# Attention scores with the keys in the partitions: four heads in row bands of TensorE, sums and outputs in column bands

## The chip, the cores and the metric

The kernel runs on one core of a Trainium2 chip. The metric is the device time of one execution in microseconds (us). Engines: PE is TensorE (matrix products), PEld its weight loads, DVE is VectorE, ACT is ScalarE, POOL is GpSimd, SP issues DMAs. Each engine works through its own queue in order, and semaphores tie the queues together.

## The reference

Input `x` is 4 x 2048 rows of 512, `ctx` 4 x 77 rows of 384.

```python
q = (layernorm(x) @ Wq + bq)        # 16 heads of 32
k = ctx @ Wk + bk;  v = ctx @ Wv + bv
attn = softmax(q @ k.T / sqrt(32))   # per head, over the 77 keys
out = attn @ v                       # back to 512 columns
x = x + relu(out @ W1 + b1) @ W2 + b2
# then: layernorm, one of 8 experts by argmax of logits, gelu MLP of that expert, added to x
```

All is fp32. Most products are made in three TensorE passes: each operand is split into a rounded part (high, type fp32r) and the rest (low), and high x high, high x low and low x high are added in PSUM.

## The kernel before

The 8192 rows are worked in 16 blocks of 512 (b = 0 to 15), each as 4 sub-blocks of 128 rows (s). A list of steps, `sched`, is written out by hand; every engine walks it and issues what the step holds for it, so this list sets the order in every queue. PSUM has 8 banks; a program gives each step of PE the bank that is free longest, and `own_bank` makes PE wait until that bank's last reader is done.

In a block, XT transposes the normalised rows, Q makes the queries with features in the partitions (4 tiles m of 128 features, which are 4 heads each, so a group g of heads is a tile), S makes scores for a group and a sub-block with 128 rows in the partitions and 4 x 77 = 308 columns, against a block-diagonal key tile `kbd`. DVE takes the maxima; ACT makes exponentials with the sum (groups 0 and 2), or DVE subtracts and ACT makes them at once (1 and 3). DVE takes sums and a reciprocal of 16 columns, POOL multiplies. PT transposes the probabilities with PE in 5 chunks for a pair of groups, ACT and DVE split them into high and low, and AV multiplies them with a block-diagonal `vbd`; OUT splits the result into `actA`. H and Y are the two products of the MLP (H in 8 tiles m of 12 matmuls; Y of one sub-block in two halves, YA and Y, of 12 matmuls each). TT transposes the result rows of the block before for its expert logits.

The scores of block b + 1 lie in the order between the halves of Y of block b, and PT, AV and H of a block follow after them. After the 16 blocks the experts' stage works through 71 tiles of 128 rows; the change doesn't touch it.

Of the kernel before, what the change touches and what calls it, by code (L numbers as in the profile page):

```python
# [18 lines left out]
F32 = mybir.dt.float32  # L19
# [33 lines left out]
PH = 2 * HG  # L53
CH = [128, 128, 128, 128, 104]
NC = len(CH)
VR = [min(P, NB * M - i) for i in range(0, NB * M, P)]
NV = len(VR)
CA, CC, CB = (0, 1), (2,), (3, 4)
# [9 lines left out]
PIECES = []  # L68
for _h in range(PH):
    for _c in range(NC):  # L70
        _a, _z = max(M * _h, P * _c), min(M * _h + M, P * _c + CH[_c])
        if _a < _z:
            PIECES.append((_c, _a - P * _c, _a - M * _h, _z - _a, _h))


def xattn_moe_kernel(nc, A, out):
    region = nc.dram_tensor("region", [NE * REG + P, ROW], F32).ap()
    k_parts = nc.dram_tensor("k_parts", [P, 2, KD, NB * M], F32).ap()
    v_parts = nc.dram_tensor("v_parts", [NB * M, 2, D], F32).ap()
# [26 lines left out]
    vbd, vbd_at = sb("vbd", [P, 2, NP, NC, P], F32R)  # L106
    kbd, _ = sb("kbd", [P, 2, KD, SCP], F32R)
    E, E_at = sb("E", [P, NP, SUB, 2 * SC])
# [20 lines left out]
    mx, _ = sb("mx", [P, KD * SUB, HG])  # L129
    sm, _ = sb("sm", [P, KD, SUB * HG])  # L130
    rc, _ = sb("rc", [P, KD, SUB * HG])
# [26 lines left out]
    def staged(name, shape, dt=F32):  # L158
# [6 lines left out]
    assert o[0] <= E_at + size([P, KD, SUB, SC], F32)  # L165
# [3 lines left out]
    v_f = [staged(f"v_f{i}", [P, D]) for i in range(2)]  # L169
# [3 lines left out]
    k_hl = staged("k_hl", [P, 2, KD, NB * M], F32R)  # L173
    k_f = staged("k_f", [P, KD, NB * M])
    assert o[0] <= actH_at + size([P, 2, SLOTS, BLK], F32)
# [3 lines left out]
    assert NV == 3 and VR[0] >= M  # L179
    v_hl = [at(f"v_hl{i}", [P, 2, D], F32R, (rows_at[1], xn_at)[i // 2] + i % 2 * size([P, 2, D], F32))  # L180
            for i in range(NV)]
    assert 2 * size([P, 2, D], F32) <= min(size([P, SUB, ROW], F32), SUB * size([P, D], F32))
# [5 lines left out]
    b2e = at("b2e", [P, NE, D], F32, vbd_at)  # L188
    assert 4 * NE * D <= size([P, 2, KD, SCP], F32) + size([P, 2, NP, NC, P], F32)
# [28 lines left out]
    assert o[0] <= E_at + size([P, KD, SUB, SC], F32)  # L218
# [25 lines left out]
    with ExitStack() as ctx:  # L244
        bank = [ctx.enter_context(nc.psum_tensor(f"bank{i}", [P, 512], F32)) for i in range(8)]

        def sem(name):
# [7 lines left out]
        st_k, st_v, ld_k, ld_v = sem("st_k"), sem("st_v"), sem("ld_k"), sem("ld_v")  # L255
# [7 lines left out]
            "dve_bks pe_k act_kf act_k dve_k pe_v dve_vf act_v dve_v pool_zero dve_const "  # L263
            "act_wq dve_wq act_w1 pool_w1 act_w2 dve_w2 act_kbd dve_tri "
            "dve_xn pool_xb pe_xT act_xT dve_xT pe_q act_q dve_q pe_s dve_max dve_sub act_es act_exp dve_rc pool_p "
            "pe_pt act_pt dve_pt pe_av act_c dve_c act_o dve_o pe_h act_h dve_h pe_y dve_x2 dve_row pool_ones pe_gate dve_gate "
# [12 lines left out]
        def attention_tail(b):  # L279

            for c in range(NC):
                step("PT", b, 0, c)
            if b:
                step("SUM", b, KD - 1)
            for c in CA:
                step("PT", b, 1, c)
            if b:
                step("TT", b - 1, 0)  # L290
            step("AV", b, 0, "C")
            step("COPY", b, 0)
            step("AV", b, 0, "A")
            step("AV", b, 0, "B")
            if b:
                step("TT", b - 1, 1)
            step("AV", b, 1, "A")
            step("ADD", b, 0, "A")
            step("ADD", b, 0, "B")
            step("OUT", b, 0, "A")  # L300
            for c in CC + CB:
                step("PT", b, 1, c)
            if b:
                step("TT", b - 1, 2)
            step("AV", b, 1, "C")
            step("OUT", b, 0, "B")
            step("COPY", b, 1)
            step("AV", b, 1, "B")
            step("ADD", b, 1, "A")
            step("ADD", b, 1, "B")  # L310
            step("OUT", b, 1, "A")
            step("OUT", b, 1, "B")
            if b:
                for s in range(SUB - 1):
                    step("TTOUT", b - 1, s)
            else:
                for i in (1, 2):
                    step("VHI", i)
                for i in (1, 2):
                    step("VLO", i)  # L320
                    step("VSTORE", i)

# [4 lines left out]
        step("BKS")  # L327
        step("DRAIN")
# [6 lines left out]
        step("KP", 3)  # L335
        for m in range(KD):
            step("KLO", m)
        step("KSTORE")
# [3 lines left out]
        step("KCOPY")  # L342
# [4 lines left out]
        step("VHI", 0)  # L347
        step("VLO", 0)
        step("VLOAD", 0, 0)
        step("VLOAD", 0, 1)  # L350
        step("VSTORE", 0)
        step("CONV_W1", 0)
        step("Q", 0, 1)


        for s in range(SUB - 1):
            step("S", 0, 0, s)
        step("QLO", 0, 1)
        step("Q", 0, 2)
        step("S", 0, 0, SUB - 1)  # L360
        step("CONV_W1", 1)
        for s in range(SUB):
            step("S", 0, 1, s)
        step("QLO", 0, 2)
        step("EXP", 0, 1)
        step("Q", 0, 3)
        step("SUM", 0, 0)
        for s in range(SUB):
            step("S", 0, 2, s)
        step("QLO", 0, 3)  # L370
        step("VP", 1)
        step("SUM", 0, 1)
        for s in range(SUB):
            step("S", 0, 3, s)
        step("EXP", 0, 3)
        step("VP", 2)
        step("VF", 1)
        step("SUM", 0, 2)
        step("VF", 2)
        step("SUM", 0, 3)  # L380
        step("XLOAD", 0)


        for b in range(NBLK):
            last = b == NBLK - 1
            if (b + 1) % BPB == 0 and not last:
                step("KLOAD", (b + 1) // BPB)
            attention_tail(b)

            values = (b + 1) // BPB if (b + 1) % BPB == 0 and not last else None  # L390
# [12 lines left out]
            for m in range(MF):  # L403
                step("H", b, m)
# [17 lines left out]
                if b and m == 0:  # L422
                    step("TT", b - 1, SUB - 1)
                    step("TTOUT", b - 1, SUB - 1)
# [8 lines left out]
                if values is not None and m == 0:  # L433
                    step("VLOAD", values, 0)
# [9 lines left out]
                if b and m == ranks:  # L444
                    for s in range(SUB):
                        step("SCAT", b - 1, s)
                    if not last:
                        step("XLOAD", b + 1)
                    if values is not None:
                        step("VLOAD", values, 1)  # L450
# [4 lines left out]
                if b == 0 and m == 2:  # L455
                    for s in range(SUB):
                        step("XB", 0, s)
                    step("ZERO_ROWS")
                    step("EB1_LOAD")
                    step("XLOAD", 1)  # L460
# [19 lines left out]
            else:  # L480
# [11 lines left out]
                if prep is not None:  # L492
                    step("E2_RAW", prep)
                    step("E1_RAW", prep)
                step("Y", b, 1)

                for m in range(2):
                    step("Q", b + 1, m)
                    step("QLO", b + 1, m)
                if prep is not None:  # L500
                    step("E2_HIGH", prep)
                for g, (first, y) in enumerate((("YA", 2), ("Y", 2), ("YA", 3), ("Y", 3))):
                    for s in range(SUB):
                        step("S", b + 1, g, s)
                    if prep is not None and g == 0:
                        step("E2_LOW", prep)
                        step("E2_STORE", prep)
                    step("EXP", b + 1, g)
                    if g:
                        step("SUM", b + 1, g - 1)  # L510
                    step(first, b, y)
                    if g + 2 < KD:
                        step("Q", b + 1, g + 2)
                        step("QLO", b + 1, g + 2)
# [21 lines left out]
        ON_ACT = (0, 2)  # L536
        ON_DVE = tuple(g for g in range(KD) if g not in ON_ACT)

        def score_done(b, g, s):

            mine, name = (ON_ACT, "act_es") if g in ON_ACT else (ON_DVE, "dve_sub")
            return S[name], SUB * (len(mine) * b + mine.index(g)) + s + 1


        def group_of(p, i):

            return 2 * p + (i == "B")

        freed = {
            "KP": lambda m: (S["act_kf"], m + 1),  # L550
            "VP": lambda i: (S["dve_vf"], i + 1),
            "XT": lambda b, s: (S["dve_xT"], SUB * b + s + 1),
            "Q": lambda b, m: (S["dve_q"], KD * b + m + 1),
            "S": lambda b, g, s: score_done(b, g, s),
            "PT": lambda b, p, c: (S["dve_pt"], NC * (NP * b + p) + c + 1),
            "AV": lambda b, p, i: (S["act_c"], NP * b + p + 1) if i == "C" else (S["dve_o"], KD * b + group_of(p, i) + 1),
# [58 lines left out]

        chains = []

        DRIP = {"QLO": 2, "PT": 2, "Y": 1, "TTOUT": 1}

        def drip(n):  # L620
            while chains and n > 0:
# [50 lines left out]
        def sp_xnload(sp, b, s0):  # L672
            for s in (s0, s0 + 1):
                if b:
                    sp.wait_ge(S["pe_xT"], SUB * (b - 1) + s + 1)
                if b == 1:
                    sp.wait_ge(st_v, 16 * NV)
# [1207 lines left out]
```

## Time and profile before

| what | value |
|---|---|
| median of three runs | 1459.77 us (1459.54 to 1459.94) |
| the profiled execution: its own time / its span | 1461.93 us / 1460.1 us |
| busy: PE, PEld, DVE, ACT, POOL | 99%, 82%, 71%, 52%, 28% of the span |
| share of PE in the chain that ended last | 96% |
| mean granted clock of PE | 0.998 of full speed |

The chain that ended last is followed back from the last instruction, at each step to what released it. An engine's share in it is the time that the end of the execution hung on it.

### The profile page before, as it was taken

Reading aid. Unit: us, or ns where it says so; the run is one execution under the profiler, and the core shown is the slowest. Engines: PE = TensorE matmul, PEld = TensorE weight load, DVE = VectorE, ACT = ScalarE, POOL = GpSimd, SP = SyncE. Lnnn points to the kernel's source line nnn. Section 1 sums busy time; section 2 is a strip of 40 time slices with the busy share of each in tenths; the row PEclk is TensorE's granted clock in tenths of the full one; section 3 lists DMA queues with packets and bytes.
Section 4 is the critical chain, followed back from the end, with each engine's and each line's share of the span. In section 5 each row is a group of like instructions: output and inputs, shape, how many; then the busy total and the mean of one; then the engine's idle time right before and its main releaser. Section 6 shows DMA issues by size and latency. Waiting matters only on the chain.

```text
span 1460.1 us, 23469 instructions
## 1 busy us (share of the span) xinstructions
PE 1439.2 (99%) x7704; PEld 1203.9 (82%) x7704; DVE 1037.0 (71%) x2522; ACT 756.9 (52%) x2096; POOL 416.0 (28%) x306
## 2 busy tenths in 40 slices
PE   8999999999999999999999999999999999999997
PEld 6788887888788888888787888888887878788996
DVE  6768586776868685867768685858576675748666
ACT  6746353645445363536454453635363544547885
POOL 3422222212121312222221213122222213108875
PEclk9999999999999999999999999999999999999999
DMA  8210202121120303130211201130202012357984
GB/s 294 85 58 1 88 1 73 38 79 55 36 88 22 102 7 103 28 99 30 81 43 37 87 23 58 43 91 1 87 1 87 1 44 73 145 174 255 305 257 149
DMA packets 70339, 121.60 MB, mean 83 GB/s; under 512 B 21851, under 2 KB 30308, under 8 KB 69197
## 3 DMA queue, kind: packets, MB, share of 16 engines
q1 hardware_dynamic: 59421, 86.41, 19.5%
q0 software_dynamic: 10800, 33.70, 6.0%
q8 instruction: 65, 1.06, 0.3%
q14 instruction: 53, 0.43, 0.1%
HBM read 75.19 MB, written 46.40 MB: 83 GB/s over the span
## 4 chain that ended last, share of the span: by engine, by line
PE 96%; DVE 2%; ACT 1%; issue 1%; DMA 0%; POOLq 0%; POOL 0%; SPq 0%; DVEq 0%
PE bank L1201 24%; PE bank L1223 24%; PE bank L1016 12%; PE bank L1153 8%; PE bank L1042 7%; PE bank L1623 4%; PE bank L1117 4%; PE bank L1661 3%; PE bank L1607 2%; PE bank L1298 2%; PE bank L984 2%; PE bank L1276 1%; DVE actH L1134 1%; ACT actH L1128 1%; PE bank L847 1%
## 5 line engine op out<-in xcount | busy, mean ns | idle before, releaser
L1223 PE MATMUL bank<-w,actH 128*128 128x512 f32 x1536 | 372.1, 393 | 0.0
L1201 PE MATMUL bank<-actA,w 128*128 128x512 f32 x1536 | 370.4, 394 | 0.0
L1201 PEld LDWEIGHTS bank<-actA,w 128*128 128x128 f32 x1536 | 284.2, 188 | 61.0
L1223 PEld LDWEIGHTS bank<-w,actH 128*128 128x128 f32 x1536 | 283.0, 188 | 55.9
L1111 POOL TENSOR_TENSOR E<-E,rc 128x1232 f32<-128x1232 f32 x64 | 144.1, 2252 | 423.3 <-DVE rc L1105 423.3
L1373 POOL DMA_INDIRECT region<-rows,pos x64 | 63.7, 996 | 456.6 <-DVE pos L1367 418.2
L1208 ACT ACTIVATE actH<-bank,b 128x512 fp32r<-128x512 f32 x128 | 88.4, 691 | 189.4 <-PE bank L1201 189.4
L1016 PE MATMUL bank<-actA,wq 128*128 128x512 f32 x768 | 182.4, 390 | 0.0
L1084 ACT ACTIVATE E<-bank,mx 128x77 f32<-128x77 f32 x512 | 157.8, 362 | 34.9 <-DVE mx L1051 34.9
L1016 PEld LDWEIGHTS bank<-actA,wq 128*128 128x128 f32 x768 | 144.1, 188 | 30.3 <-issue 0.5
L1030 DVE SCALAR_TENSOR_TENSOR actQ<-bank,bq,actQ 128x512 fp32r<-128x512 f32 x64 | 48.0, 750 | 158.5 <-ACT actQ L1025 158.5
L1213 DVE TENSOR_TENSOR actH<-bank,actH 128x512 fp32r<-128x512 f32 x128 | 88.2, 689 | 55.7 <-ACT bank L1209 55.0
L1153 PE MATMUL bank<-actH,vbd 128*128 128x512 f32 (+1 forms) x480 | 122.0, 400 | 4.2 <-DVE actH L1134 4.2
L1084 ACT ACTIVATION_READ_ACCUMULATOR E<-bank,mx 128x1 f32 x512 | 124.5, 243 | 0.0
L1042 PE MATMUL bank<-kbd,actQ 128*128 128x308 f32 x768 | 118.7, 303 | 0.0
L1042 PEld LDWEIGHTS bank<-kbd,actQ 128*128 128x128 f32 x768 | 113.9, 188 | 5.7 <-issue 0.5
L1051 DVE TENSOR_REDUCE mx<-bank 128x4 f32<-128x308 f32 x256 | 110.4, 471 | 6.8 <-PE bank L1042 6.8
L1025 ACT ACTIVATE actQ<-bank,bq 128x512 fp32r<-128x512 f32 x64 | 44.1, 689 | 125.1 <-PE bank L1016 125.0
L1153 PEld LDWEIGHTS bank<-actH,vbd 128*128 128x128 f32 (+1 forms) x480 | 86.5, 188 | 25.7 <-DVE actH L1134 6.9
L1134 DVE TENSOR_TENSOR actH<-bank,actH 128x512 fp32r<-128x512 f32 (+1 forms) x160 | 98.7, 676 | 11.5 <-ACT actH L1128 11.5
L1006 POOL TENSOR_TENSOR rows<-rows,b2bc 128x512 f32<-128x512 f32 x64 | 84.7, 1335 | 52.5 <-DMA rows<-in_x 43.7
L989 ACT ACTIVATE actA<-bank 128x512 fp32r<-128x512 f32 x64 | 34.7, 596 | 107.7 <-PE bank L984 107.7
(172 smaller groups left out, 2108.3 us busy)
## 6 DMA issues: line engine op xcount, KB each, us to landing
rowB<-region SPq DMA_DIRECT2D x71, 258.0 KB
xn<-in_x SPq DMA_DIRECT2D x64, 256.0 KB, 2.9
rows<-in_x SPq DMA_DIRECT2D x64, 256.0 KB, 3.5
w_raw<-in_W SPq DMA_DIRECT2D x2, 2048.0 KB, 10.5
e_raw<-in_E SPq DMA_DIRECT2D x16, 256.0 KB, 3.2
region<-padrow SPq DMA_DIRECT2D x9, 258.0 KB, 2.2
e_parts<-e_high SPq DMA_DIRECT2D x8, 256.0 KB, 2.0
e_parts<-e_low SPq DMA_DIRECT2D x8, 256.0 KB, 2.3
```

Of the source, the lines that this page charges most:

```text
L1006: nc.gpsimd.tensor_tensor(r, r, b2bc[:], ALU.add).then_inc(S["pool_xb"], 1)
L1016: mm = pe.matmul(p[:], w, a, start=k == 0 and j == 0, stop=k == KD - 1 and j == 2)
L1042: mm = pe.matmul(p[:, 0:SC], q, k, start=j == 0, stop=j == 2)
L1051: dve.tensor_reduce(mx[:, SUB * g + s, :], p, AX, ALU.max, negate=True).then_inc(S["dve_max"], 1)
L1084: ins = act.activation(probs(g)[:, s, M * h:M * h + M], of("S", b, g, s)[:, M * h:M * h + M], ACT.Exp, bias=mx[:, SUB * g + s, h:h + 1], a ...
L1111: nc.gpsimd.tensor_tensor(e, e, r, ALU.mult).then_inc(S["pool_p"], 1)
L1134: dve.tensor_tensor(actH[0:CH[c], 1, j % SLOTS, :], of("PT", b, pr, c)[0:CH[c], :], f32(actH[0:CH[c], 0, j % SLOTS, :]), ALU.subtract).the ...
L1153: mm = pe.matmul(p[:], v, w, start=c == mine[0] and t == 0, stop=c == mine[-1] and t == 2)
L1201: mm = pe.matmul(p[:], w, a, start=k == 0 and j == 0, stop=k == KD - 1 and j == 2)
L1208: act.activation(actH[:, 0, m, :], p[:], ACT.Relu, bias=b1[:, m:m + 1])
L1213: dve.tensor_tensor(actH[:, 1, m, :], of("H", b, m)[:], f32(actH[:, 0, m, :]), ALU.subtract).then_inc(S["dve_h"], 1)
L1223: mm = pe.matmul(p[:], a, w, start=m == 0 and j == 0, stop=m == MF - 1 and j == 2)
```

## The change

Scores are now made with the keys in the partitions. For each group of 4 heads:

- SM: one pass of high query x high key, as before with rows in the partitions; DVE takes the negated maxima from it, only to keep the exponents small. MT transposes the maxima of two groups with PE, and ACT copies them to `mT`.
- ST: for each head, 77 keys (and one row more) x 512 rows, from the head's 32 features in 32 rows of the array: three products and a fourth, with a selecting matrix `sel`, that adds the maximum. The 4 heads lie in 4 bands of 32 rows and write 4 banks.
- EXP: ACT makes the exponentials of 77 x 512, head by head.
- SUMS and AV: plain fp32 products of the exponentials with ones, and with the values `vt`; each head writes 32 of the 128 PSUM partitions, a band of 32 columns of the array.
- RC and NORM: DVE takes the reciprocal of the sums, 128 x 512, and multiplies. OUT: ACT rounds, and POOL (group 3: DVE) takes the rest.

PT, the block-diagonal `vbd`, its splits, the key and value pieces that DMAs put in place and POOL's multiply are gone. Y(b, 1) moves behind the queries of the next block, and the first two tiles of H are now made side by side, step HK by step over k.

```diff
-        def pe_s(pe, b, g, s):
-            for j, (q, k) in enumerate(split3([actQ[:, h, g, P * s:P * s + P] for h in range(2)],
-                                              [kbd[:, h, g, 0:SC] for h in range(2)])):
-                mm = pe.matmul(p[:, 0:SC], q, k, start=j == 0, stop=j == 2)
...
+        def pe_sm(pe, b, g, s):
...
+            pe.matmul(p[:, 0:SC], actQ[:, 0, g, P * s:P * s + P], kbd[:, g, 0:SC], start=True, stop=True
+                      ).then_inc(S["pe_sm"], 1)
...
+        def pe_st(pe, b, g, h):
+            own_bank(pe, "ST", b, g, h)
+            if h < HG - 1:
+                return
+            pe.wait_ge(S["dve_q"], KD * b + g + 1)
+            pe.wait_ge(S["act_mt"], NP * b + g // 2 + 1)
...
+            for j, (k, q) in enumerate(split3([k_hl[:, x, g, i:i + KS] for x in range(2)],
+                                              [actQ[:, x, g, :] for x in range(2)]) + ((sel[:, g % 2, :], mT[:]),)):
+                for h in range(HG):
+                    r = slice(HD * h, HD * h + HD)
+                    mm = pe.matmul(of("ST", b, g, h)[0:KS, :], k[r], q[r], start=j == 0, stop=j == 3)
...
+        def act_exp(act, b, g, h):
+            n = KD * b + g
+            act.wait_ge(S["pe_s"], n + 1)
+            if n >= 2:
+                act.wait_ge(S["pe_av"], n - 1)
+            act.activation(E[0:M, g % 2, h, :], of("ST", b, g, h)[0:M, :], ACT.Exp).then_inc(S["act_exp"], 1)
+
+        def by_columns(pe, p, b, g, held):
+            for h in range(HG):
+                r = slice(HD * h, HD * h + HD)
+                mm = pe.matmul(p[r, :], held(h), E[0:M, g % 2, h, :], start=True, stop=True)
+            return mm
+
+        def pe_sums(pe, b, g):
+            p = own_bank(pe, "SUMS", b, g)
+            pe.wait_ge(S["act_exp"], HG * (KD * b + g + 1))
...
+            by_columns(pe, p, b, g, lambda h: one[0:M, :]).then_inc(S["pe_sums"], 1)
+
+        def dve_rc(dve, b, g):
+            dve.wait_ge(S["pe_sums"], KD * b + g + 1)
+            if g:
+                dve.wait_ge(S["pool_o"], (KD - 1) * b + g)
+            dve.reciprocal(att[:], of("SUMS", b, g)[:]).then_inc(S["dve_rc"], 1)
...
+            by_columns(pe, p, b, g, lambda h: vt[0:M, P * g + HD * h:P * g + HD * h + HD]).then_inc(S["pe_av"], 1)
+
+        def dve_norm(dve, b, g):
...
+            dve.tensor_tensor(att[:], of("AV", b, g)[:], att[:], ALU.mult
+                              ).then_inc(S["dve_n"], 1)
+
+        def act_out(act, b, g):
...
+            act.wait_ge(S["dve_n"], KD * b + g + 1)
+            act.activation(actA[:, 0, g, :], att[:], ACT.Identity).then_inc(S["act_o"], 1)
```

On PE before, from the last transposes XT of block b + 1 (`xn`) to AV (`vbd`): Y is `w_51`, Q is `wq`, S is `kbd`, PT is `ident,E`, TT `ident,rows`.

```order
L984 MATMUL bank<-ident,xn_65 128x128 x4
L1223 MATMUL bank<-w_51,actH 128x512 x12
L1016 MATMUL bank<-actA,wq 128x512 x24
L1042 MATMUL bank<-kbd,actQ 128x308 x12
L1223 MATMUL bank<-w_51,actH 128x512 x12
L1016 MATMUL bank<-actA,wq 128x512 x12
...
L1117 MATMUL bank<-ident,E 128x128 x8
L1276 MATMUL bank<-ident,rows_59 128x128 x4
L1153 MATMUL bank<-actH,vbd 128x512 x15
```

On PE in the change, the same stretch, from XT to the loop of the groups: SM is `kbd`, MT `ident,mx`, ST `k_hl` and `sel`, SUMS `E,one`, AV `E,vt`.

```order
L932 MATMUL bank<-ident,xn_71 128x128 x4
L964 MATMUL bank<-actA,wq 128x512 x24
L989 MATMUL bank<-kbd,actQ 128x308 x4
...
L1048 MATMUL bank<-E,one 32x512 x4
L1048 MATMUL bank<-E,vt 32x512 x4
L1034 MATMUL bank<-actQ,k_hl 78x512 x12
L1034 MATMUL bank<-mT,sel 78x512 x4
L1008 MATMUL bank<-ident,mx 128x128 x4
L1148 MATMUL bank<-w_51,actH 128x512 x12
```

Q now stands directly behind XT, with no half of Y between them. A loop SUMS(g), AV(g), ST(g + 1), half of Y comes three times in a block (MT in the first alone), then SUMS(3) and AV(3).

On ACT in the change, a part of the same loop (EXP is `E`, OUT is `att`), with what each instruction waits for:

```order
L1042 ACTIVATE E_58<-bank0 77x512 [waits pe_av,pe_s]
L1042 ACTIVATE E_58<-bank5 77x512 [waits pe_av,pe_s]
L1338 ACTIVATE e2_high_159<-e2_raw_157 128x512 [waits ld_e2raw]
L1083 ACTIVATE actA_52<-att_63 128x512 [waits dve_n,pe_q]
L1042 ACTIVATE E_58<-bank5 77x512 [waits pe_av,pe_s]
L1042 ACTIVATE E_58<-bank1 77x512 [waits pe_av,pe_s]
```

OUT of a group, which waits for DVE's product (`dve_n`), stands ahead of the exponentials of the next group.

## Rows read from the trace of the kernel before

**Rows 1.** The page: busy time of each engine, and the chain by engine.
```profile
PE 1439.2 (99%) x7704; PEld 1203.9 (82%) x7704; DVE 1037.0 (71%) x2522; ACT 756.9 (52%) x2096; POOL 416.0 (28%) x306
...
PE 96%; DVE 2%; ACT 1%; issue 1%; DMA 0%; POOLq 0%; POOL 0%; SPq 0%; DVEq 0%
```

**Rows 2.** Timeline of PE in a middle block: start, length, engine, line, operation, count.
```profile
727.51 1.03 PE L984 MATMUL bank<-ident,xn 128*128 128x128 f32 x8
728.30 2.98 PE L1223 MATMUL bank<-w,actH 128*128 128x512 f32 x12
731.12 5.60 PE L1016 MATMUL bank<-actA,wq 128*128 128x512 f32 x24
736.55 1.85 PE L1042 MATMUL bank<-kbd,actQ 128*128 128x308 f32 x12
738.24 2.92 PE L1223 MATMUL bank<-w,actH 128*128 128x512 f32 x12
741.00 2.88 PE L1016 MATMUL bank<-actA,wq 128*128 128x512 f32 x12
...
757.02 2.93 PE L1223 MATMUL bank<-w,actH 128*128 128x512 f32 x12
759.79 3.22 PE L1117 MATMUL bank<-ident,E 128*128 128x128 f32 x28
762.84 0.60 PE L1276 MATMUL bank<-ident,rows 128*128 128x128 f32 x4
...
770.79 2.31 PE L1153 MATMUL bank<-actH,vbd 128*128 128x512 f32 x9 [0.20 <-DVE actH L1134]
772.94 3.36 PE L1201 MATMUL bank<-actA,w 128*128 128x512 f32 x14
```

**Rows 3.** Busy time by stretch (us, then each engine, PE's clock): a block, the end.
```profile
760.00:840.12 80.12, 79.92 (x416) 66.64 (x415) 59.36 (x150) 38.92 (x113) 18.10 (x13) 1.00 0.18 57
1450.00:1460.00 10.00, 2.83 (x14) 1.70 (x12) 5.58 (x10) 0.93 (x4) 4.92 (x5) 0.73 0.06 18
```

**Rows 4.** Timeline of all engines, around XT: ACT copies, DVE splits.
```profile
728.14 1.09 ACT L989 ACTIVATE actA<-bank 128x512 fp32r<-128x512 f32 x2 [2.54 <-PE bank L984]
728.77 1.29 DVE L996 TENSOR_TENSOR actA<-bank,actA 128x512 fp32r<-128x512 f32 x2 [2.09 <-ACT actA L989]
```

**Rows 5.** Timeline of PEld in the first block: weight loads of a plain fp32 product.
```profile
36.00 0.19 PEld L872 LDWEIGHTS bank<-wv_raw,ctxT 128*128 128x128 f32 x1 [0.24 <-issue]
36.43 0.19 PEld L872 LDWEIGHTS bank<-wv_raw,ctxT 128*128 128x128 f32 x1 [0.24 <-issue]
```

**Rows 6.** Groups by line and shape: busy us, mean ns of one, idle before.
```profile
L872 PE MATMUL bank<-wv_raw,ctxT 128*128 128x512 f32 x12 | 5.5, 592 | 0.0
L1105 DVE RECIPROCAL rc<-sm 128x16 f32<-128x16 f32 x64 | 15.9, 249 | 1.1
L1257 DVE RECIPROCAL rows<-r 128x4 f32<-128x4 f32 x16 | 2.9, 180 | 0.5
L1178 DVE TENSOR_TENSOR actA<-bank,actA 128x512 fp32r<-128x512 f32 x64 | 44.1, 689 | 0.5
L1162 ACT ACTIVATE csb<-bank 128x512 f32<-128x512 f32 x32 | 19.2, 600 | 12.2 <-PE bank L1153 12.2
```

**Rows 7.** Timeline of ACT and DVE in the tail of a block.
```profile
760.42 3.52 ACT L1128 ACTIVATE actH<-bank 128x512 fp32r<-128x512 f32 x7
...
767.94 0.60 ACT L1173 ACTIVATE actA<-bank 128x512 fp32r<-128x512 f32 x1 [3.03 <-DVE bank L1169]
768.57 0.69 DVE L1178 TENSOR_TENSOR actA<-bank,actA 128x512 fp32r<-128x512 f32 x1
```

**Rows 8.** Timeline of PE in the first block: from Q to H.
```profile
18.91 6.02 PE L1016 MATMUL bank<-actA,wq 128*128 128x512 f32 x24
...
56.11 8.10 PE L1201 MATMUL bank<-actA,w 128*128 128x512 f32 x35
```

**Rows 9.** Waits: engine, line, released by: us in total, times, longest.
```profile
POOL E L1111 <- DVE rc L1105: 423.3, 62, 19.1
```

More of the change, by code:

```diff
@@ L52 @@
 NP = KD // 2
[L53 to L58, printed above, removed]
+KS = M + 1
+KW = (NB * M + 1 + 7) // 8 * 8
 SLOTS = 8
@@ L277, in step, with maxima, scores, exponentials @@
             sched.append((kind, *i))
[L279 to L321, printed above, removed]
+        def maxima(b, g):
+            for s in range(SUB):
+                step("SM", b, g, s)
+        def scores(b, g):
+            for h in range(HG):
+                step("ST", b, g, h)
+        def exponentials(b, g):
+            for h in range(HG):
+                step("EXP", b, g, h)
+        def outputs(b, g):
+            step("SUMS", b, g)
+            step("RC", b, g)
+            step("AV", b, g)
+            step("NORM", b, g)
+            step("OUT", b, g)
         step("SETUP")
@@ L364, in xattn_moe_kernel @@
[L364 to L381, printed above, removed]
+        maxima(0, 1)
@@ new lines, in xattn_moe_kernel @@
+        step("QLO", 0, 2)
+        step("Q", 0, 3)
+        step("MT", 0, 0)
+        maxima(0, 2)
+        step("QLO", 0, 3)
+        scores(0, 0)
+        exponentials(0, 0)
+        step("VP", 1)
+        maxima(0, 3)
+        step("VF", 1)
+        step("VSTORE", 1)
+        outputs(0, 0)
+        scores(0, 1)
+        exponentials(0, 1)
+        step("MT", 0, 1)
+        step("VP", 2)
+        step("VF", 2)
+        step("VSTORE", 2)
+        outputs(0, 1)
+        scores(0, 2)
+        exponentials(0, 2)
@@ L384, in xattn_moe_kernel @@
+        step("CONV_W1", 1)
+        step("VP", 3)
+        step("VF", 3)
+        step("VSTORE", 3)
+        outputs(0, 2)
+        scores(0, 3)
+        exponentials(0, 3)
         for b in range(NBLK):
             last = b == NBLK - 1
[L386 to L390, printed above, removed]
+            context = (b + 1) // BPB if (b + 1) % BPB == 0 and not last else None
+            if context is not None:
+                step("KCOPY", context)
+            g = KD - 1
+            if b:
+                step("SUMS", b, g)
+                step("RC", b, g)
+                step("AV", b, g)
+                for s in range(SUB - 1):
+                    step("TT", b - 1, s)
+                step("NORM", b, g)
+                step("TTOUT", b - 1, 0)
+                step("OUT", b, g)
+                step("TTOUT", b - 1, 1)
+                step("TTOUT", b - 1, 2)
+            for m in range(2):
+                step("H", b, m)
+            step("HK", b, 0)
+            step("HK", b, 1)
+            if b == 0:
+                outputs(b, g)
+            step("HK", b, 2)
+            if b:
+                step("TT", b - 1, SUB - 1)
+                step("TTOUT", b - 1, SUB - 1)
+            step("HK", b, 3)
@@ L432, in xattn_moe_kernel @@
                     step("XNLOAD", b + 1, 2)
-                if values is not None and m == 0:
-                    step("VLOAD", values, 0)
+                if context is not None and m == 0:
+                    step("VLOAD", context)
                 if not last and m == 3 and prep is not None:
@@ L1181, in pe_h @@
[L1181 to L1195 removed]
+                pe.wait_ge(S["act_q"], KD * b + g + 1)
```

472 lines of the change are left out of this document (185 added, 287 removed).

## The prediction

> **What bounds the kernel now.** I read the page first: PE is busy 99% of the span, and 96% of the chain that ended last is PE [rows 1]. A reader should see that no other engine can be worth anything here unless PE comes to wait for it; the longest wait of the list is POOL's for DVE, 423 us in all, and costs nothing [rows 9]. Then the timeline of PE in one block: its pieces join without a gap, apart from 0.20 us before the last AV [rows 2]. A block is 80.1 us, with DVE busy 59 of them and ACT 39 [rows 3]. So the question is what PE does for attention in a block, before and after, and whether it starts to wait.
>
> **Attention on PE before.** S: 12 matmuls from 736.55 to 738.24 are 1.69 us, four times 6.76. From 759.79 (PT) to 772.94 (H) are 13.15 us, of which 12 matmuls are TT; a transpose costs 3.05 / 28 = 0.109 (759.79 to 762.84), so 1.31 for TT and 11.84 for PT and AV [rows 2]. Together **18.6 us** a block. A 512-column pass costs 0.23 (2.76 for 12, 738.24 to 741.00) [rows 2].
>
> **After, the pieces with a row.** SM: 16 passes of 1.69 / 12 = 0.141, 2.25 us. MT: 8 transposes, 0.87. Q now stands right behind XT. Before, a half of Y lay there: PE left XT at 728.30 and took up Y, while ACT's copies and DVE's splits of XT ran to 728.77 + 1.29 = 730.06 [rows 2, 4]. That half of Y is now behind Q, so PE waits about **1.8 us** a block.
>
> **The pieces without a row.** No matmul of before works in bands next to another, so both ends:
> - ST, 16 passes per group in four row bands: 16 x 0.23 = 3.68 us if one after the other, 0.92 if four at once. I take 0.92: neighbours in the queue are different heads, different rows, different banks, and nothing ties them. A block makes four groups.
> - SUMS and AV, 4 fp32 products each per group. An fp32 product is two loads and two passes: the 6 products of the value projection left 12 records, 0.43 us from load to load, 592 ns each [rows 5, 6]. So 16 passes are 6.88 us per group if serial, and 1.72 if four bands run at once. But the two passes of a product lie next to each other in the queue and use the same band: the second must wait for the first, and the next head's first pass stands behind it. If passes start in the order of the queue, each start moves on by one pass per head: 8 products start 0.43 apart, the last takes two passes, 9 x 0.43 = **3.87 us**. I take this one. Until the sums alone are ready: 1.02 (one pass and one 592 ns record), 2.31 or 3.60 us, for full, in order and serial.
> - The reciprocal of 128 x 512: DVE took 180 ns for 4 columns and 249 for 16 [rows 6], 5.75 ns a column, so 249 + 496 x 5.75 = **3.10 us**. The lower bound is the nearest 512-column row of DVE, 0.69 [rows 6]. I take 3.10: this is the same instruction. The Trainium skill (VectorE: DVE Perf Modes, "First, the fixed hardware budget") says that a reciprocal repeats its divide steps 8 times; with the page's 0.96 GHz that would be an estimated 8 cycles, 8.3 ns a column, and 4.3 us. The rows show 5.75; by the page the sum below would be 56 us longer.
> - An exponential of 77 x 512: as a copy of 128 x 512, 600 ns [rows 6]; in a run they follow each other at (3.52 - 0.60) / 6 = 0.49 [rows 7].
>
> **The loop that decides.** From SUMS(g) to SUMS(g + 1) hangs a chain through three engines: the sums are ready (2.31), RC 3.10, NORM 0.69 [rows 6], OUT on ACT, and only behind OUT, in ACT's queue, the four exponentials of the next group, which SUMS(g + 1) waits for. OUT and four exponentials are 4 x 0.49 + 0.60 = 2.55. A hop between engines is some 0.03 (ACT ends 768.54, DVE starts 768.57) [rows 7]; four at 0.04 are 0.16. Without the sums the chain is 6.50 us, so the loop takes **8.8 us** (full bands 7.5, serial 10.1). In the same time PE has SUMS and AV 3.87, ST 0.92, half of Y 2.76: 7.55 us. PE waits 1.25 us, three times a block. With full bands its work is 5.40 and it waits 2.1; with serial ones it has 10.56 and doesn't wait. ST(g + 1) ends before OUT(g) in each case, so the exponentials wait for OUT and not for PE. POOL's part of OUT, which RC of the next group waits for, is done within those exponentials (POOL waits most of its time as it is).
>
> **The sum.** Per block from 1 to 15: SM 2.25, MT(0) 0.44, ST(0) 0.92, SUMS(3) and AV(3) 3.87, three loops 26.4 less the three halves of Y in them, 8.28, and Q's wait 1.8: 27.4, so **+8.8 us**, 132 for 15. After SUMS(3) nothing waits: the way to OUT(3) through RC, NORM, ACT and DVE is some 7.6 us, under which PE has AV, 16 transposes and 18 matmuls of H. Block 0 has nothing to fill its loops with but value projections. Q starts at 18.9 as before [rows 8]; Q, SM, MT and ST bring PE to 33.2, the exponentials, a projection and SM to 36.3, three loops to 62.7, and the last part of H, behind OUT(3), ends at about 71.6. Before, H began at 56.11 and its first 24 matmuls ended at 61.6 [rows 8]. That is +10. Together **+142 us**.
>
> Costed at nothing: the DMAs of keys and values (no piece of PE in these rows waits for one), POOL's multiply [rows 9], and DVE's load: it loses splits, subtractions, sums and additions of some 18.6 us a block and gains 15, under PE's longer block. ACT gains slack too. If a cover is gone it shows as a longer loop, at three times its size per block. The profiled execution's own time is 1461.9, 2.2 above the median; 1461.9 + 142 is 1604, on the median's scale **1602 us**.
>
> **The rivals.**
> - *Full bands.* The two passes of a product don't hold up the next head. Per block 2.25 + 0.44 + 0.92 + 1.72 + 22.5 - 8.28 + 1.8, and 0.35 because DVE's maxima of group 3 delay RC(0): 21.7, +3.1; block 0 +5. +51, 1511 us: slower still, because the loop is bound by the reciprocal and PE waits 6 us a block. For it: the bands read and write apart. Against it: the queue's order. The Trainium skill (TensorE: Matmul & The Clock Gate, Part 3) gives 2.38 times for three column bands and 3.07 for four row bands; an estimate from that, some 3.2 for four columns, is 2.2 us per group, and the time near 1520. No run here shows it. Chance 0.25.
> - *Column bands serial.* Loops of 10.56, SUMS and AV 6.88: 36.2, +17.6 a block, +16 in block 0: +279, 1739 us. For it: all bands share rows 0 to 76. Chance 0.14.
> - *No bands at all*, so that the change doesn't do what it says: 2.25 + 0.87 + 4 x (3.68 + 6.88) + 1.8 = 47.2, +28.6 a block: +454, 1914 us. Chance 0.07.
> - *A quick reciprocal with full bands*: the other side. With RC at 0.69 the loop is 5.1 and PE's own 5.40 bounds it: 2.25 + 0.87 + 4 x (0.92 + 1.72) + 1.8 = 15.5, -3.1 a block and -4 in block 0: -51, 1409 us. It decides from about 2.0 us for RC down. Against it: two lengths of the same instruction on one line. Chance 0.10.
> - *A reciprocal steeper than its line*: from 16 to 512 columns the row gives no point between. At a third more, 4.3 us, each loop is 1.2 longer: 3.5 a block, +56: 1658 us. Chance 0.05.
>
> **The numbers.** Forecast 0.37, rivals 0.25, 0.14, 0.07, 0.10 and 0.05, and 0.02 that pieces cancel to nothing. The range from 1495 to 1745 holds the forecast, full bands, serial columns and the steeper reciprocal, 0.81, and leaves out the quick reciprocal and no bands. Within 0.2% is about what a measurement of this kernel can't tell from no change. Faster 0.10, same 0.02, slower 0.88.
>
> **What would show it.** A reciprocal of 128 x 512 near 3.1 us; weight loads of SUMS and AV 0.43 apart in pairs that overlap, 9 x 0.43 from the first to the last; PE idle before SUMS(1), (2), (3), released by ACT's exponentials, 1.2 us each; PE idle about 1.8 us before Q, released by DVE; a block of 89 us. Wrong it would be with a short reciprocal, with bands other than in order, or if PE's clock falls: in these rows it is 1.00, the 2.4 GHz level, with gaps of 0.2 us, and 0.73 in the last 10 us, when PE stood idle for most [rows 3]. At 1.2 GHz each pass takes twice as long.

## The result, and the profile after

The changed kernel takes **1562.18 us** (median of four runs, 1561.75 to 1563.81), the kernel before, in runs beside it, 1459.86 us. The ratio is 1.0703, with a 95% interval from 1.0685 to 1.0722: 7% slower. The prediction was 1602 us in a range from 1495 to 1745.

The page of the changed kernel: busy time of each engine, the clock granted to PE in 40 slices, the chain by engine, and the group of the reciprocal.

```profile
PE 1445.3 (93%) x8254; PEld 1064.9 (68%) x8254; DVE 1013.9 (65%) x2155; ACT 613.4 (39%) x1145; POOL 330.3 (21%) x292
...
PEclk9799999999999989999999989999999999999999
...
PE 72%; DVE 16%; ACT 6%; issue 3%; DMA 1%; SPq 1%; POOL 0%; ACTq 0%; POOLq 0%; DVEq 0%
...
L1063 DVE RECIPROCAL att<-bank 128x512 f32<-128x512 f32 x64 | 214.7, 3355 | 115.4 <-PE bank L1048 115.4
```

Beside [rows 1] one line says most: PE was 96% of the chain and is 72%, and DVE and ACT have come into it. They are less busy than before, so it is not their load that bounds; PE waits for something that passes through them. What it waits for is in the list of PE's waits (us in total, times, longest):

```profile
PE bank L1048 <- ACT E L1042: 71.0, 44, 2.6
PE bank L964 <- DVE actA L944: 25.0, 15, 1.7
```

L1048 is SUMS and AV, L1042 the exponentials, L964 is Q. The timeline of PE in a middle block has the places:

```profile
791.28 5.69 PE L964 MATMUL bank<-actA,wq 128*128 128x512 f32 x24 [1.66 <-DVE actA L944]
...
811.86 1.06 PE L1048 MATMUL bank<-E,one 77*32 77x512 f32 x8
812.74 1.04 PE L1048 MATMUL bank<-E,vt 77*32 77x512 f32 x8
813.71 0.94 PE L1034 MATMUL bank<-actQ,k_hl 32*78 32x512 f32 x12
...
815.22 2.98 PE L1148 MATMUL bank<-w,actH 128*128 128x512 f32 x12
820.04 1.06 PE L1048 MATMUL bank<-E,one 77*32 77x512 f32 x8 [1.84 <-ACT E L1042]
820.90 1.38 PE L1048 MATMUL bank<-E,vt 77*32 77x512 f32 x8
822.21 1.57 PE L1034 MATMUL bank<-actQ,k_hl 32*78 32x512 f32 x12
...
828.12 1.06 PE L1048 MATMUL bank<-E,one 77*32 77x512 f32 x8 [0.61 <-ACT E L1042]
...
836.20 1.06 PE L1048 MATMUL bank<-E,one 77*32 77x512 f32 x8 [2.10 <-ACT E L1042]
...
876.83 3.42 PE L964 MATMUL bank<-actA,wq 128*128 128x512 f32 x14 [1.66 <-DVE actA L944]
```

Three things are to be seen. The sums come 8.18, 8.08 and 8.08 us apart, and PE waits before each. The column bands work at once: 8 passes of the sums, from 811.86 to 812.74, are 0.88 us, and those of AV 0.97. At 812.0 to 812.2, before any second pass has begun, four passes are running:

```profile
811.86 0.64 PE L1048 MATMUL bank<-E,one 77*32 77x512 f32 x4
```

And in the second loop the same passes take longer than in the first: the scores 1.57 us instead of 0.94. The windows of these places (length, busy time of each engine, PE's clock, DMA) show why, with the block above and the one after it:

```profile
821.00:824.60 3.60, 3.60 (x29) 1.38 (x22) 3.36 (x1) 0.00 (x0) 0.00 (x0) 0.57 0.47 146
...
791.28:876.83 85.55, 79.33 (x448) 57.37 (x449) 58.18 (x126) 29.39 (x52) 12.99 (x12) 0.98 0.17 53
876.83:964.92 88.09, 82.47 (x448) 59.36 (x449) 58.18 (x126) 29.38 (x52) 13.08 (x12) 0.94 0.17 56
```

After the idle 1.84 us the granted clock is 0.57, most of it at the 1.2 GHz level. In the loops most of this is hidden, since PE would wait anyway. In two of the 15 blocks, of which the second row is one, it falls where PE has no slack, and the block takes 2.5 us more. Before, a block took 80.12 us at clock 1.00 [rows 3].

How a loop hangs together is read from the chain of work between two SUMS (start, length, what; the small pieces between are issue):

```profile
813.17 3.28 DVE att L1063
...
816.54 0.70 DVE att L1076
...
817.33 0.04 ACT actA L1083
...
817.87 2.04 ACT E L1042 x4
819.90 0.14 issue
820.04 1.10 PE bank L1048 x8
```

Reciprocal, NORM, OUT (of which only the start counts, 0.54 us till the first exponential), four exponentials, sums. ScalarE had been free for long when it came to OUT: its row in the timeline of all engines says what it waited for, with the scores of the next group ready since about 814.8.

```profile
817.33 0.63 ACT L1083 ACTIVATE actA<-att 128x512 fp32r<-128x512 f32 x1 [6.30 <-DVE att L1076]
```

Where the span's 100.3 us (1560.4 against 1460.1) come from, by the starts of Q in the two traces: Q of block 0 starts at 21.77 instead of 18.91, 2.9 later; Q of block 1 at 105.21 instead of 91.08, 11.3 more; Q of block 15 at 1306.09 instead of 1210.02, 81.9 more in 14 blocks, 5.85 each; from there to the experts' stage 6.7 more; that stage itself is 2.5 shorter. The 2.9 us at the start were no term of the prediction. The timeline of DVE and PE there:

```profile
9.64 0.37 DVE L763 TENSOR_REDUCE lg<-ident 128x32 f32<-128x128 f32 x1 [6.88 <-DMA ident<-in_ident]
...
10.27 2.46 DVE L915 BATCH_NORM_STATS2 bn<-xn 128x6 f32<-128x512 f32 x4
...
16.26 1.94 PE L932 MATMUL bank<-ident,xn 128*128 128x128 f32 x16 [1.64 <-DVE xn L921]
```

The new step SEL, which reads the identity, stands ahead of the statistics of `xn` in DVE's queue and waits for the identity's DMA; the transposes wait 1.64 us for DVE. The other 1.2 us come from PE itself: it was through with the key products ahead of the transposes at 14.6, where before the transposes began at 13.44.

### The profile page after: what moved, and what is told of

Read it like the earlier page. It is cut to its first block, busy times and chain, and to the rows that moved or that the text cites. A ratio compares the mean times of both kernels' runs of the same rounds, so it can differ in the third digit from the quotient of the medians.

```text
span 1560.4 us, 23319 instructions
## 1 busy us (share of the span) xinstructions
PE 1445.3 (93%) x8254; PEld 1064.9 (68%) x8254; DVE 1013.9 (65%) x2155; ACT 613.4 (39%) x1145; POOL 330.3 (21%) x292
## 4 chain that ended last, share of the span: by engine, by line
PE 72%; DVE 16%; ACT 6%; issue 3%; DMA 1%; SPq 1%; POOL 0%; ACTq 0%; POOLq 0%; DVEq 0%
PE bank L1123 23%; PE bank L1148 16%; PE bank L964 11%; DVE att L1063 10%; ACT E L1042 6%; PE bank L1048 5%; PE bank L1548 3%; PE bank L1586 2%; PE bank L1201 2%; DVE att L1076 2%; PE bank L1223 2%; PE bank L989 2%; DVE mx L1002 2%; PE bank L1034 2%; PE bank L1532 1%
## 5 line engine op out<-in xcount | busy, mean ns | idle before, releaser
L1148 PE MATMUL bank<-w,actH 128*128 128x512 f32 x1536 | 389.3, 405 | 0.0
L1148 PEld LDWEIGHTS bank<-w,actH 128*128 128x128 f32 x1536 | 291.4, 195 | 81.9 <-issue 23.2
L1063 DVE RECIPROCAL att<-bank 128x512 f32<-128x512 f32 x64 | 214.7, 3355 | 115.4 <-PE bank L1048 115.4
L964 PE MATMUL bank<-actA,wq 128*128 128x512 f32 x768 | 184.2, 392 | 25.0 <-DVE actA L944 25.0
L1089 POOL TENSOR_TENSOR actA<-att,actA 128x512 fp32r<-128x512 f32 x48 | 61.2, 1275 | 616.6 <-ACT actA L1083 616.6
L964 PEld LDWEIGHTS bank<-actA,wq 128*128 128x128 f32 x768 | 141.5, 188 | 55.5 <-issue 28.6
L1083 ACT ACTIVATE actA<-att 128x512 fp32r<-128x512 f32 x64 | 40.4, 632 | 313.0 <-DVE att L1076 313.0
L1042 ACT ACTIVATE E<-bank 77x512 f32<-77x512 f32 x256 | 130.1, 587 | 57.1 <-PE bank L1034 57.1
L1048 PE MATMUL bank<-E,one 77*32 77x512 f32 x512 | 68.2, 602 | 71.0 <-ACT E L1042 71.0
L1166 DVE TENSOR_TENSOR rows<-bank,rows 128x512 f32<-128x512 f32 x64 | 44.3, 692 | 64.3 <-PE bank L1148 64.2
L1134 ACT ACTIVATE bank<-bank,b 128x512 f32<-128x512 f32 x128 | 83.8, 655 | 0.0
L1638 POOL DMA_INDIRECT out<-rowB x71 | 70.5, 994 | 23.8 <-issue 9.3
```

Of the source, the lines that this page charges most:

```text
L964: mm = pe.matmul(p[:], w, a, start=k == 0 and j == 0, stop=k == KD - 1 and j == 2)
L1042: act.activation(E[0:M, g % 2, h, :], of("ST", b, g, h)[0:M, :], ACT.Exp).then_inc(S["act_exp"], 1)
L1048: mm = pe.matmul(p[r, :], held(h), E[0:M, g % 2, h, :], start=True, stop=True)
L1063: dve.reciprocal(att[:], of("SUMS", b, g)[:]).then_inc(S["dve_rc"], 1)
L1134: act.activation(p[:], p[:], ACT.Relu, bias=b1[:, m:m + 1]).then_inc(S["act_h"], 1)
L1148: mm = pe.matmul(p[:], a, w, start=m == 0 and j == 0, stop=m == MF - 1 and j == 2)
```

## The experiments

The runs were made on several chips; each ratio is to the kernel before on the same chip, where that took between 1459.6 and 1464.5 us.

**e1: OUT behind the next exponentials.** In `outputs(b, g)` the last step goes, and it comes back after the exponentials:

```diff
     step("NORM", b, g)
-    step("OUT", b, g)
...
     exponentials(b + 1, 1)
+    step("OUT", b + 1, 0)
```

> The step OUT(b,g) of groups 0 to 2 is put behind the four exponentials of group g+1, in the queues of ScalarE and GpSimd; nothing else changes. Theory: ScalarE's queue closes the loop. OUT(g) waits for NORM(g), so for the reciprocal of 3.36 us, and the exponentials of g+1 stand behind it although their scores are ready (the scores end at 814.80 in the middle block, the exponentials start at 817.87). Then TensorE's idle time before the sums falls from 71.0 us to under 25; the next limit is the single buffer att (reciprocal 3.36, NORM 0.69, copy 0.63, GpSimd's difference 1.27, and steps between, about 6.3 us), near TensorE's own work of 6.3 us in a loop, so the sums come 6.3 to 6.7 us apart instead of 8.1, and the kernel takes 1485 to 1515 us. Rival: the reciprocal, or the buffer behind it, sets the 8.1 us by itself: the sums stay over 7.6 us apart, and the time is within 15 us of 1562.

1464.84 us, ratio 1.0000 (0.9990 to 1.0009): the whole loss is gone. PE's wait for the exponentials is no longer in the list, the wait before Q is unchanged, and the block is PE's again. First the longest waits of PE, then the loop in the timeline of all engines, then the window of that block:

```profile
PE bank L970 <- DVE actA L950: 25.0, 15, 1.7
PE bank L821 <- DMA wk_raw<-in_Wk: 6.9, 1, 6.9
...
758.01 3.35 DVE L1069 RECIPROCAL att<-bank 128x512 f32<-128x512 f32 x1
...
759.85 2.05 ACT L1048 ACTIVATE E<-bank 77x512 f32<-77x512 f32 x4 [3.90 <-PE bank L1040]
...
762.25 0.63 ACT L1089 ACTIVATE actA<-att 128x512 fp32r<-128x512 f32 x1 [0.35 <-DVE att L1082]
...
763.05 1.06 PE L1054 MATMUL bank<-E,one 77*32 77x512 f32 x8
...
768.92 1.07 PE L1054 MATMUL bank<-E,one 77*32 77x512 f32 x8
...
736.20:815.72 79.52, 77.83 (x448) 56.51 (x449) 57.98 (x126) 29.61 (x52) 12.38 (x11) 1.00 0.18 57
```

The exponentials now run beside the reciprocal, and the next sums come 5.87 us after the last. The rival falls. The expected 1485 to 1515 was too high, since it counted the idle 71.0 us alone: with the gaps the slow passes went too. PE's busy time fell from 1445.3 to 1411.7 us for the same 8254 instructions, 33.6 us; with 71.0 that is 104.6, and 7.03% of 1460 is 102.6. This doesn't make 33.6 us the price of the clock: in the loops the slow passes only filled time in which PE would have waited (e7 has the clock by itself).

**e2: a copy in place of the reciprocal.**

```diff
-dve.reciprocal(att[:], of("SUMS", b, g)[:])
+dve.tensor_copy(att[:], of("SUMS", b, g)[:])
```

> The reciprocal of the sums (128x512) is replaced by a plain copy of the same tile, so the division is left out of the computation; the order of all steps stays. Theory: the reciprocal's 3.36 us stand in the loop sums, reciprocal, NORM, OUT, exponentials, sums. A copy of this shape takes about 0.7 us, the loop becomes 8.1 less 2.7, 5.4 us, under TensorE's own 6.3 us, the idle time before the sums (71.0 us) goes almost wholly, and with it the stretches at half clock behind it: 1475 to 1495 us. Rival: the loop is held by something that has no reciprocal in it (a bank, GpSimd's difference, a wait of ScalarE for scores): under 20 us.

1454.49 us, ratio 0.9934 (0.9917 to 0.9950). The copy took 681 ns, the loop no longer holds PE, and the block is 79.25 us at clock 1.00. It breaks the same chain at another place, so the reciprocal and the place of OUT are one cause, not two. The expectation was too high again, for the reason given at e1. The kernel leaves the division out; it is a probe of time alone.

**e3: XT ahead of the half of Y.**

```diff
-for s in range(2):
+for s in range(SUB):
     step("XT", b + 1, s)
 step("YA", b, 1)
-for s in range(2, SUB):
-    step("XT", b + 1, s)
```

> The transposes XT of subtiles 2 and 3 are put ahead of the first half of Y of subtile 1, which then lies between the transposes and Q. Theory: the 1.66 us that TensorE idles ahead of Q, 25.0 us in 15 blocks, are the copy and the difference of the last transposes, and 2.9 us of products laid between cover most of it: the wait falls to under 0.6 us, the time to 1540 to 1549 us. Rival: the normalised rows of subtiles 2 and 3 or a free bank come later than the transposes now stand, so the wait only moves ahead of the transposes: the time is within 6 us of 1562.

A miss: four runs between 1549.34 and 1574.18 us, median 1566.13, too far apart for a ratio. The wait before Q did vanish from the list, but the sums still wait 74.2 us, and the clock falls more often. Two of its blocks:

```profile
440.44:524.00 83.56, 78.97 (x449) 57.57 (x448) 58.09 (x126) 29.24 (x52) 12.46 (x12) 0.98 0.17 54
779.73:867.59 87.86, 83.92 (x449) 59.81 (x448) 58.09 (x126) 29.25 (x52) 13.28 (x13) 0.92 0.16 52
```

The first is 2 us shorter than a block of the changed kernel, as the theory has it; the second does the same work and is longer, at clock 0.92. Whether the move gains a little alone is not shown by runs this far apart. The rival falls too, since nothing waits ahead of XT.

**e4: heads in the outer loop of the scores** (`products` stands for the three of `split3` and the one with `sel`).

```diff
-for j, (k, q) in enumerate(products):
-    for h in range(HG):
+for h in range(HG):
+    for j, (k, q) in enumerate(products):
```

> In the scores of a group the loop over the four heads (row bands) becomes the outer one, the four products of a head the inner one: TensorE's queue then holds four passes of one band, four of the next, and so on. Theory 1: TensorE works through passes in the order of its queue and one that needs a busy band holds up those behind it, as the prediction's likeliest case had it. Then 13 of 16 passes follow one another: the group takes about 13 times 0.22, 2.9 us, instead of 1.10; 1.8 us more in a block at the first group (the loops of the others have as much idle time): 1585 to 1605 us. Theory 2: each band takes its own passes from the queue as it comes free: the group stays at 1.0 to 1.3 us and the time within 6 us of 1562.

1572.75 us, ratio 1.0738 (1.0720 to 1.0756), 0.3% above the changed kernel's. The scores of a group, in PE's timeline:

```profile
812.52 0.95 PE L1034 MATMUL bank<-actQ,k_hl 32*78 32x512 f32 x12
813.27 0.43 PE L1034 MATMUL bank<-mT,sel 32*78 32x512 f32 x4
813.63 3.02 PE L1148 MATMUL bank<-w,actH 128*128 128x512 f32 x12
```

1.11 us until Y begins, against 1.09 with the heads inside. Theory 1 wanted 2.9 and falls. The time is over what theory 2 allowed: of 9.6 us more in the span, 4.0 lie in the experts' stage, and the rest goes with the clock, which fell in other blocks than before (one of 89.36 us, one of 88.18).

**e5: e1 and e3 together**, no other edit.

> Two moves together: OUT(b,g) behind the exponentials of group g+1, and XT of subtiles 2 and 3 ahead of the first half of Y of subtile 1. With the first alone the block was 79.55 us and TensorE still waited 1.66 us ahead of each Q (25.0 us in all) at full clock; with the second alone that wait was gone, but the clock fell more often. Theory: what made the second move worthless was the idle time in the loops, through the clock; without it the move brings its 25 us. Block 77.8 to 78.2 us, clock at 0.99 or over, 1436 to 1446 us, faster than the kernel before the change. Rival: the second move itself costs (the exponentials or the banks come later), so the block stays over 79 us and the time at 1455 to 1470.

1431.92 us, ratio 0.9807 (0.9791 to 0.9824). What gave no clear gain with the idle loops in place gains 28 us without them (ratios 1.0000 and 0.9807). A middle block is 77.60 us; it and the time are slightly under what was expected.

**e6: e5, and SEL later, and NORM into a free tile of E.**

```diff
-step("SEL")                       # ahead of the first normalisation
 step("CONV_WQ", 1)
+step("SEL")
...
-    dve.wait_ge(S["pool_o"], (KD - 1) * b + g)
+    dve.wait_ge(S["dve_n"], KD * b + g)
     dve.reciprocal(att[:], of("SUMS", b, g)[:])
...
-dve.tensor_tensor(att[:], of("AV", b, g)[:], att[:], ALU.mult)
+dve.tensor_tensor(E[:, g % 2, HG - 1, :], of("AV", b, g)[:], att[:], ALU.mult)
```

OUT and the differences read that tile too, and the exponential that overwrites it waits for them.

> The two moves of the run beside it, and two more: the step SEL stands behind CONV_WQ(1) in VectorE's queue instead of ahead of the first normalisation, and NORM writes into the fourth head's tile of E (free by then) instead of att, so that the reciprocal of the next group waits for NORM alone and not for GpSimd's difference. Theory: the first Q started 2.9 us later than before the change because SEL waits for the identity's load; it starts at 18.5 to 19.5 us now. The buffer att holds block 0 alone, where no products of Y cover it: the first block (first Q to second) falls from 78.4 to 70 to 74 us, the middle blocks don't move. Together 6 to 10 us under the run beside it: 1428 to 1438 us. Rival for SEL: the first normalisation waits for its rows and not for SEL, so Q starts at 21.7 as in the changed kernel; rival for att: block 0 is held by VectorE's reciprocals or the conversion of W1, so it stays over 76 us.

1422.92 us, ratio 0.9748 (0.9732 to 0.9765): the fastest of all, 2.5% under the kernel before, and 9.0 us under e5, as expected. Q of block 0 starts at 19.70 instead of 21.62 in e5, a little later than expected: the normalised rows are ready as early as before, and what is left, 0.8 us beside 18.91, is the key products ahead of the transposes. Block 0 is 73.06 us instead of 76.54; middle blocks move by 0.2. The page's busy times, and the window of a middle block:

```profile
PE 1401.8 (99%) x8254; PEld 1043.6 (73%) x8254; DVE 1009.6 (71%) x2155; ACT 616.4 (43%) x1145; POOL 331.1 (23%) x292
...
711.18:788.51 77.33, 77.33 (x449) 56.50 (x448) 57.91 (x126) 29.62 (x52) 12.30 (x11) 1.00 0.19 59
```

PE has no idle time left in the block. Beside 80.12 us before [rows 3], 2.8 us a block is what the new form of attention is worth to PE, once nothing holds it up.

**e7: the gaps filled with dropped products.**

```diff
 p = own_bank(pe, "SUMS", b, g)
+if b and g:
+    for _ in range(5):
+        pe.matmul(p[:], w1[:, 0, 0, 0:P], w2[:, 0, 0, :], start=True, stop=True)
 pe.wait_ge(S["act_exp"], HG * (KD * b + g + 1))
```

> The changed kernel with five more products (128x512 of w1 and w2, 0.23 us each) ahead of the wait for the exponentials, into the bank of the sums, which the real sums then overwrite; in the 45 loops of blocks 1 to 15, so the kernel does more work and computes the same. Theory: TensorE's clock falls to about half behind the idle gaps; with 1.15 us of each gap filled it stays up: span clock 0.98 or over instead of 0.97, the second half of the loop at full clock. The loop stays at 8.1 us, because the chain through the reciprocal sets it and not TensorE; only the two blocks of 88.1 us come back to 85.5: 1550 to 1562 us. Rival: the clock falls for another reason than the gaps (it is the products in bands themselves that lower it): the span's clock stays at 0.97 or lower, and the added products cost time, 1562 to 1580 us.

1552.39 us, ratio 1.0638 (1.0620 to 1.0656): more work, and 0.6% less time than the changed kernel's 1.0703. The loop in PE's timeline, and the window of the block:

```profile
815.59 1.06 PE L1048 MATMUL bank<-E,one 77*32 77x512 f32 x8 [0.61 <-ACT E L1042]
816.48 1.04 PE L1048 MATMUL bank<-E,vt 77*32 77x512 f32 x8
817.45 0.93 PE L1034 MATMUL bank<-actQ,k_hl 32*78 32x512 f32 x12
...
823.59 1.07 PE L1048 MATMUL bank<-E,one 77*32 77x512 f32 x8 [0.89 <-ACT E L1042]
...
786.92:872.22 85.30, 81.22 (x464) 59.30 (x464) 58.22 (x126) 29.35 (x52) 12.85 (x11) 1.00 0.16 53
```

The clock stays at 1.00 and the scores at 0.93, so it was the gaps that lowered it. But the sums still come 8.0 us apart: the chain sets the loop, not PE, and the clock alone cost only some 10 us.

**e8 and e10: more products in one band.** Both are e6 with dropped products of head 0 ahead of the four: three in each group in e8, and as many as the group's number, 0 to 3, in e10.

```diff
-for h in range(HG):
+for h in (0, 0, 0) + tuple(range(HG)):     # e8
+for h in (0,) * g + tuple(range(HG)):      # e10
```

> On the kernel of e6_out_xt_sel_norm (1422.9 us): ahead of the four products of a group's sums stand three more products of head 0 into the same band of columns, overwritten by the fourth; the same for the outputs. So band 0 has 8 passes in a row in each, the others 2 as before, and the result is the same. Theory: each band works by itself and a pass of fp32 with 512 columns holds its band for 0.43 us. Then the passes of bands 1 to 3 start within 0.1 us of the first, ahead of passes that stand before them in the queue, and sums and outputs of a group take 16 times 0.43, 6.9 us, instead of 1.85: 5 us for each of 64 groups, 1730 to 1775 us, which is what one band alone would cost. Rival, as the prediction's likeliest case had it: TensorE keeps to the order of its queue, and bands 1 to 3 start only 2.6 us after band 0, when its first three products are through.

> As e8_band0_times4, but with none, one, two and three more products of band 0 ahead in groups 0, 1, 2 and 3, so 2, 4, 6 and 8 passes of band 0 stand ahead of those of bands 1 to 3. Theory from that run: a band holds one running pass and three waiting ones, and only what is beyond these holds up the queue. Then bands 1 to 3 start with the first pass of band 0 in groups 0 and 1, 0.86 us later in group 2 and 1.72 us later in group 3; the time, 10 us more in each block, is 1575 to 1600 us. Rival: each product of a band lets the queue go on one pass of 0.43 later or more, so bands 1 to 3 start late in group 1 too.

e8, one run: 1749.27 us. The total is as expected: sums and outputs of a group are 6.98 us long (911.31 to 918.29), the block 97.86, 5.1 more for each of its four groups. That is the price of one band alone. Of the starts, both theories missed: the others begin with the fifth pass of band 0, 1.74 us late. PE's timeline at three instants (each row shows the passes then running, from the start of the first):

```profile
911.31 3.62 PE L1057 MATMUL bank<-E,one 77*32 77x512 f32 x14
...
912.62 0.59 PE L1057 MATMUL bank<-E,one 77*32 77x512 f32 x1
...
912.62 1.07 PE L1057 MATMUL bank<-E,one 77*32 77x512 f32 x5
```

At 913.0 a single pass runs, at 913.09 four more. A band takes one pass in 0.43 us, so three of these belong to bands 1 to 3, and band 0 still has three to start, which stand ahead of them in the queue. The theory formed from this was put to e10 (one run, 1585.38 us, in the range given). Instants after the first pass in its groups 1, 2 and 3, with 4, 6 and 8 passes of band 0 ahead:

```profile
825.73 0.64 PE L1057 MATMUL bank<-E,one 77*32 77x512 f32 x4
...
833.78 0.59 PE L1057 MATMUL bank<-E,one 77*32 77x512 f32 x1
833.78 1.06 PE L1057 MATMUL bank<-E,one 77*32 77x512 f32 x5
...
843.93 1.07 PE L1057 MATMUL bank<-E,one 77*32 77x512 f32 x5
```

In group 1 all four bands run from the first moment. In group 2, whose sums begin at 833.33, the others join between 834.15 and 834.25, some 0.9 us later; in group 3, from 842.62, between 844.3 and 844.4, some 1.75 us. As expected: one pass of a band may run and three wait, and only what is beyond these holds up the queue. The rival, with a late start in group 1 too, falls. In e4 four passes of each row band stood in a row and held up nothing, which agrees.

**e9: att freed early, OUT left where it is.** The edit of NORM from e6 alone, on the changed kernel.

> The changed kernel with one edit: NORM writes into the fourth head's tile of E instead of att, so that the next reciprocal need not wait for OUT and GpSimd's difference; ScalarE's order stays (OUT ahead of the next exponentials). Theory: the loop of 8.1 us runs through ScalarE's queue, and the buffer att with its 6.3 us lies inside it: the loops stay at 8.0 to 8.2 us, the middle blocks at 85.0 to 86.0, TensorE's idle time before the sums at 60 to 80 us; the time is 1550 to 1566 us, with what is gained in block 0 alone. Rival: moving OUT behind the exponentials helped because it changed when att comes free; then freeing att by itself gives most of it too: under 1520 us.

1566.93 us, ratio 1.0706 (1.0680 to 1.0732), the changed kernel's own. PE's wait for the exponentials is 69.8 us, and in a middle block the sums still come 8.18, 8.08 and 8.08 us apart (815.37, 823.55, 831.63, 839.71). The buffer is not what holds the loop; block 0, at 83.48 us, gained nothing either. In e6, where OUT is out of the way, block 0 is 3.5 us shorter; the move of SEL was made with it there, so that this is the buffer's doing is likely, but not shown by itself.

## Why the prediction was right, and where it was not

**Right: what bounds, and why.** The loop through reciprocal, NORM, OUT and, behind OUT in ACT's queue, the exponentials sets the time. It shows in the chain, and e1 and e2 each break it at one place and take back the whole loss. The prediction gave 7.5 us for it with full bands and 8.8 in order; it is 8.1. Q's wait, 1.8 in the prediction, is 1.66, released by DVE. That nothing of the old work is missed (DMAs, POOL) holds.

**Wrong: the step that the prediction leaned on.** "If passes start in the order of the queue, each start moves on by one pass per head": this gave 3.87 us for SUMS and AV of a group, and they take 1.85, near the 1.72 of full bands. The first passes of the four heads start together, although each head's second pass stands between them in the queue. In its place e8 and e10 show that up to three passes of a busy band can wait without holding up the others; the change puts only two of a band in a row, so it never gets there. The Trainium skill (TensorE: Matmul & The Clock Gate, Part 3, "The mechanism") says that matmuls start and end strictly in the order of the program. Rows of e10 differ for the starts. For the end of a group e8 agrees: the reciprocal starts after the last pass of band 0, though bands 1 to 3 are through before.

```profile
915.02 3.36 DVE L1072 RECIPROCAL att<-bank 128x512 f32<-128x512 f32 x1 [2.39 <-PE bank L1057]
```

So the rival of full bands came about, at 1562 us instead of its 1511. That the forecast of 1602 came within 40 us is partly luck: its 3.87 us for the bands were too much by 2, while other terms were too small, and the range held the result because it was drawn to take in this rival. What was mis-sized in the rival:

- The **reciprocal** was set at 3.10 us and takes 3.355. From 16 columns on [rows 6] that is (3355 - 249) / 496 = 6.26 ns a column, not 5.75. The Trainium skill's eight repeats (VectorE: DVE Perf Modes, "First, the fixed hardware budget") gave an estimate of 4.3 us; the trace lies nearer to the line through the short rows.
- The **loop**, 8.08 instead of 7.5: 0.25 by the reciprocal, 0.1 until the sums are ready (820.04 to 821.16), and 0.2 in the hops between engines.
- The **clock**. The prediction named a fall as what would make it wrong and set no price. It fell after the gaps, in two blocks where PE had no slack, 2.5 us each; e7 gives 10 us in all.
- The **start**, 2.9 us, was not counted. SEL's wait for the identity is 1.6 us of it on PE, since the order of DVE's queue ahead of the first normalisation was not gone through; taking SEL away gave 1.9 in e6. Why the key products ahead of the transposes were later as well stays open.
- **ST** at 0.92 is 1.09 us; full bands in rows too, but not four times as fast as one.
- **Block 0** costs 11.3 instead of the 5 of that rival; moving OUT takes 5.1 of it back (e1: 78.38 us instead of 83.44).

By their sum: 14 blocks at 5.85 instead of 3.1 are 38.5 us, block 0 6.3, the last block 6.7 - 3.1 = 3.6, the start 2.9, and the experts' stage -2.5; 48.8 of the 51. Of the 2.75 in a middle block the loops are 1.7, the rest is spread over the clock and small pieces and was not taken apart.

**What stays open.** Why the clock fell oftener in e3 and e4 than in the changed kernel, with the idle time before the sums nearly the same, no run shows.

## What to carry to other kernels

When a change makes one engine's work cheaper, write down the chain from one use of its product to the next through all queues, and look for an instruction that waits for a late result ahead of one that is ready: here a single 0.63 us copy ahead of the exponentials in ScalarE's queue cost 7%, and moving it cost nothing. The idle time in a list of waits can be less than what a loop loses: closing 71 us of gaps gave back 103, since passes at a lower clock had filled part of the time; the clock by itself cost some 10 (e7). And a second improvement that gains nothing clear may only be held up by the first: the move of XT gave no clear gain alone and 28 us after OUT had been moved.

## What was not expected of the hardware

- TensorE's bands take their passes out of the queue's order: with four passes of band 0 ahead, bands 1 to 3 start in the same moment; with six and eight ahead, 0.9 and 1.75 us later, with three passes of band 0 still waiting (e10).
- Four bands of columns make fp32 products almost four times as fast as one: 8 passes in 0.88 us, where one band takes 0.43 for each (e8).
- A reciprocal of 128 x 512 takes DVE 3.355 us, against 0.68 for a copy of the same shape (e2).
- The kernel with 225 more products on TensorE took 0.6% less time, with a mean granted clock of 0.995 instead of 0.971 (e7).
